# Attention over a graph: scores from turned gathered rows against 16 targets times 4 heads, turned head products kept in f32, four buffers of gathered rows

## The reference, cut to what matters

```python
h = jnp.maximum(_layernorm(x, axis=-1), 0.0)
Q = (h @ Wq).reshape(n, H, D)
K = (h @ Wk).reshape(n, H, D)
V = (h @ Wv).reshape(n, H, D)
score = jnp.einsum('ehd,ehd->eh', Q[src], K[dst]) / np.sqrt(D)
attn = jax.nn.softmax(score, axis=1)          # over the 4 heads
m = V[src] * attn[:, :, None]
h_new = jax.ops.segment_sum(m, dst, num_segments=n)
x = x + layernorm(h_new.reshape(n, H * D) @ Wo + h) * gamma + beta
```

## Time and profile before

| | us |
|---|---|
| median of 3 runs | 3534.71 |
| the runs | 3491.54, 3534.71, 3550.27 |
| profiled execution, its span | 3529.8 |
| PE / DVE / ACT / POOL busy in it | 1964.1 / 2235.0 / 1128.3 / 1615.5 |

### The profile page before, as it was taken

One profiled execution on the slowest core, in us unless ns is written; L12 is line 12 of the kernel. 1 busy time (PEld: TensorE's weight loads), 2 busy tenths in 40 slices (PEclk: granted clock), 3 DMA queues, 4 the chain that ended last, 5 costly groups with the idle time before them and its releaser, 6 DMA issues. The chain is left out here.

```text
span 3529.8 us, 59565 instructions
## 1 busy us (share of the span) xinstructions
PE 1964.1 (56%) x16222; PEld 1430.6 (41%) x16222; DVE 2235.0 (63%) x4872; ACT 1128.3 (32%) x3658; POOL 1615.5 (46%) x1665
## 2 busy tenths in 40 slices
PE   6844555555555555545766556564545445564487
PEld 5723333333333333334344435453434434554222
DVE  7877777777777777754521112134547557987899
ACT  1144555444444444533210111000001001117544
POOL 1055555555555555553666666645666562000000
PEclk9955555555555555556767677675657657985699
DMA  7912121121212222236222222215544432220000
GB/s 240 364 40 45 42 45 43 43 43 44 45 40 45 42 45 41 45 88 224 65 49 50 50 50 48 60 44 154 147 132 145 127 81 84 85 82 0 0 0 9
DMA packets 399309, 267.13 MB, mean 76 GB/s; under 512 B 321456, under 2 KB 349293, under 8 KB 399073
## 3 DMA queue, kind: packets, MB, share of 16 engines
q1 hardware_dynamic: 306278, 87.81, 11.6%
q10 hardware_dynamic: 41472, 118.96, 9.3%
q0 software_dynamic: 51488, 59.40, 6.7%
HBM read 158.59 MB, written 107.47 MB: 75 GB/s over the span
## 5 line engine op out<-in xcount | busy, mean ns | idle before, releaser
L1254 POOL DMA_INDIRECT sorted_edges<-r_load,r_to x800 | 818.6, 1023 | 544.9 <-SPq L1188 310.2
L807 POOL DMA_INDIRECT hsrc<-h,edges x808 | 775.7, 960 | 593.8 <-PE ps L1004 362.4
L1004 PE MATMUL ps<-AO,hsrc 125*64 125x64 f32 x1616 | 195.9, 316 | 309.9 <-remote 254.3
L1049 PE MATMUL ps<-hot,lo 125*128 125x400 bf16 (+2 forms) x1000 | 272.8, 455 | 100.5 <-DVE hot L866 79.9
L1004 PEld LDWEIGHTS ps<-AO,hsrc 125*64 125x64 f32 x1616 | 180.0, 224 | 345.8 <-issue 345.8
L1031 PE MATMUL ps<-rwin,there 120*125 120x256 bf16 x800 | 183.2, 404 | 235.3 <-DVE there L850 220.0
L875 DVE TENSOR_TENSOR prod<-ps,hsrc 125x1024 f32<-125x1024 f32 x200 | 244.3, 1222 | 105.1 <-issue 101.0
L1572 ACT ACTIVATE w_work<-w_work 128x384 f32<-128x384 f32 (+1 forms) x160 | 85.8, 536 | 701.5 <-DVE w_work L1773 530.4
L866 DVE TENSOR_SCALAR hot<-ramp,small 125x400 bf16<-125x400 int16 x800 | 211.9, 322 | 148.0 <-issue 142.7
L1426 PE MATMUL ps<-R 128*128 128x64 bf16 x3000 | 156.6, 218 | 184.5 <-DVE R L1762 115.9
L1031 PEld LDWEIGHTS ps<-rwin,there 120*125 120x125 bf16 x800 | 145.1, 209 | 274.1 <-issue 274.1
(11 more groups left out here) (412 smaller groups left out, 4187.1 us busy)
## 6 DMA issues: line engine op xcount, KB each, us to landing
w_work<-sorted_edges ACTq DMA_DIRECT2D x42, 1000.0 KB
r_load<-in_edge_attr_dram SPq DMA_DIRECT2D x80, 312.5 KB
dstrow<-dst_rows SPq DMA_DIRECT2D x101, 234.4 KB
sorted_edges<-A ACTq DMA_DIRECT2D x10, 2000.0 KB, 9.7
A<-counts SPq DMA_DIRECT2D x12, 1600.0 KB
counts<-A ACTq DMA_DIRECT2D x4, 4000.0 KB, 29.8
sorted_edges<-A ACTq DMA_DIRECT2D x15, 1000.0 KB, 9.5
hsrc<-h,edges POOLq DMA_INDIRECT x808
```

The source lines that it names most:

```text
L807: g.indirect_dma_start(out=hsrc[:, s, t, :], out_offset=None, in_=S.h0[:, :], in_offset=bass.IndirectOffsetOnAxis(ap=edges.bitcast(I32)[:, ...
L1004: mm = pe.matmul(sums.rearrange("d (h w) -> d h w", h=H)[:, :, OFF[t]:OFF[t] + SUB], hsrc[0:TP, s, t, :], AO[0:TP, t, :, :], start=(t == 0 ...
L1049: mm = pe.matmul(S.ps[:, at0 + c0:at0 + c1], lo[0:TP, s, t, :], hot[0:TP, t, c0 - k0:c1 - k0], start=(t == FIRST[k]), stop=False, skip_gro ...
L1254: g.indirect_dma_start(out=S.sorted, out_offset=bass.IndirectOffsetOnAxis(ap=to[:, hf, t:t + 1], axis=0), in_=load[:, hf, t, :], in_offset ...
```

## The change

- **Another way to the scores.** PE turns the gathered rows: 4 transposes of 125 x 128 (two tiles side by side, line 951 of the new program) put the 64 features of two tiles on 128 partitions. ACT copies the 500 columns from PSUM to `hT`. PE then multiplies each tile's turned rows (64 x 125 weights, on the lower or upper 64 partitions by turns) by 16 targets times 4 heads of R: 8 f32 matmuls with 64 columns (line 960). DVE picks for each edge its own target with the 0/1 position `at` (two instructions of 256 elements) and sums over 16 (one of 512 elements). `there`, `dstrow`, the products with `hsrc`, their sums, and ACT's share of them are gone.
- **R turned, in f32.** The first stage now makes R with features on partitions and nodes along the row, keeps it in f32 as `rt`, on both halves of the partitions, and does not split it.
- **Four buffers** of gathered rows, `edges` and `spot`; POOL gathers up to three items ahead. The loop bodies of all engines hold four items, so each engine jumps back 24 times.

The diff, cut:

```diff
-    rwin = sb("rwin", [KW, 2, H * D], BF16)
-    hsrc = sb("hsrc", [P, 2, T, D], F32)
-    there = sb("there", [KW, GE], BF16)
+    rwin = sb("rwin", [P, 2, H, W], F32)
+    hsrc = sb("hsrc", [P, Q, T, D], F32)
+    hT = sb("hT", [P, HT, TP], F32)
...
             with sp.Fori(0, n) as j:
-                for s in range(2):
-                    i = j * 2 + s
-                    g, b = begin(i, s)
+                for s in range(Q):
+                    i = j * Q + s
+                    b = begin(i, s)
                     sp.wait_ge(q["window_free"], i + 1)
-                    sp.dma_start(rwin[:, s, :], S.r3[bass.ds(b, W)].rearrange("n s c -> (n s) c")).then_inc(q[f"rwin{s}"], 16)
-                    line(g, i)
+                    sp.dma_start(rwin[:, s % 2, :, :], S.rt[:, :, bass.ds(b, W)]).then_inc(q[f"rwin{s % 2}"], 16)
...
-                    keys(0, 4)
-                    products(0)
-                    keys(4, 8)
-                    summed = sums(0)
...
-                    products(1)
-                    summed = sums(1)
+                    for t in range(T):
+                        v.wait_ge(q["hot_free"], T * i + t + 1)
+                        v.tensor_scalar(hot[0:TP, t, :], S.ramp[0:TP, OFF[t] * NB:OFF[t] * NB + SK], key[:, t:t + 1], None,
+                                        ALU.is_equal).then_inc(q["hot"], 1)
...
+                    v.wait_ge(q["scores"], i + 2)
+                    for r in range(2):
+                        v.tensor_tensor(prod[0:TP, r:T:2, :, :], scores_at(odd, r).rearrange("p (u h w) -> p u h w", u=HT, h=H),
+                                        at[0:TP, r:T:2, :].unsqueeze(2).to_broadcast([TP, HT, H, SUB]), ALU.mult).then_inc(q["scores_free"], 1)
+                    own.step(v.tensor_reduce(s4, prod[0:TP, :, :, :], AX.X, ALU.add))
+                    own.step(v.tensor_reduce(top, s4, AX.X, ALU.max))
...
+                    act.wait_ge(q["turned"], i + 1)
+                    act.wait_ge(q["scores"], i + 1)
+                    act.copy(hT[:, :, :], S.bank[2 + odd][:, 0:HT * TP].rearrange("p (u e) -> p u e", u=HT)).then_inc(q["moved"], 1)
...
             with pe.Fori(0, n) as j:
-                for s in range(2):
-                    pe.wait_ge(q["there"], i + 2)
...
-                        mm = pe.matmul(S.ps[0:TP, t * 256:(t + 1) * 256], there[:, t * TP:(t + 1) * TP], rwin[:, s, :],
+                for s in range(Q):
+                    for u in range(HT):
+                        if u % 2 == 0:
+                            pe.wait_ge(got[s][u // 2], j * (16 * HT) + 16 * HT)
+                        mm = pe.transpose(S.bank[2 + odd][:, u * TP:(u + 1) * TP],
+                                          hsrc[0:TP, s, 2 * u:2 * u + 2, :].rearrange("p t f -> p (t f)"), S.ident[0:TP, 0:TP])
+                    mm.then_inc(q["turned"], 1)
...
+                    pe.wait_ge(q["moved"], i + 3)
+                    for t in range(T):
+                        rows = slice(t % 2 * D, t % 2 * D + D)
+                        mm = pe.matmul(scores_at(odd, t % 2)[:, t // 2 * H * SUB:(t // 2 + 1) * H * SUB], hT[rows, t // 2, :],
+                                       rwin[rows, odd, :, OFF[t]:OFF[t] + SUB], start=True, stop=True, skip_group_check=True)
+                    mm.then_inc(q["scores"], 1)
                     pe.wait_ge(q["scores"], i + 2)
                     pe.sem_inc(q["window_free"], 1)
-                    weigh(i, 1 - s)
+                    weigh(i, (s - 1) % Q)
...
-                    act.copy(R3[:, c, 0, :], S.bank[4 + c % 3][:, 0:H * D]).then_inc(q["hi"], 1)
-                    act.wait_ge(q["rem"], c + 1)
-                    act.copy(R3[:, c, 1, :], rest[:, c % KQ, :]).then_inc(q["mid"], 1)
+                    act.copy(RT[:, :, c * P:(c + 1) * P], S.bank[4 + c % 3][:, 0:2 * P].rearrange("p (k n) -> p k n", k=2)
+                             ).then_inc(q["rt"], 1)
...
-                    pe.matmul(S.bank[4 + n % 3][:, 0:H * D], HT[0:D, n % KQ, :], Mk[0:D, :], start=True, stop=True).then_inc(q["r"], 1)
+                    for k in range(2):
+                        mm = pe.matmul(S.bank[4 + n % 3][:, k * P:(k + 1) * P], Mk[0:D, k * P:(k + 1) * P], HT[0:D, n % KQ, :],
+                                       start=True, stop=True)
```

More of the change, by code:

```diff
@@ L53 @@
 SP3 = 3
-KW = SP3 * W
+Q = 4
 KEYS = NB * W
@@ L737, in attend @@
     q = {n: sem("a_" + n) for n in (
-        "spot0", "spot1", "edges0", "edges1", "rwin0", "rwin1", "dstrow", "zero", "spot_free", "window_free",
-        "there", "lo", "squares", "lo_free", "hot", "hot_free", "scores", "scores_free", "soft", "expo", "ao", "ao_free", "carrier",
-        "edges_free", "counted", "count_free", "u", "u_free", "zeros", "proj", "proj_free", "own", "summed")}
-    got = [[sem(f"a_got{s}{t}") for t in range(T)] for s in range(2)]
-    STEPS = 10
+        "rwin0", "rwin1", "zero", "spot_free", "window_free",
+        "lo", "squares", "lo_free", "hot", "hot_free", "turned", "moved", "scores", "scores_free", "soft", "expo", "ao", "ao_free", "carrier",
+        "edges_free", "counted", "count_free", "u", "u_free", "zeros", "proj", "proj_free", "own")}
+    spotted, landed = ([sem(f"a_{n}{s}") for s in range(Q)] for n in ("spot", "edges"))
+    got = [[sem(f"a_got{s}{hf}") for hf in range(2)] for s in range(Q)]
+    STEPS = 8
     half = NB * NP // 2
@@ L835, in _ @@
             v.wait_ge(q["zero"], 5)
-            def place(own, n, s, seen):
-                v.wait_ge(q[f"spot{s}"], seen)
-                own.did(v.tensor_scalar(thr[0:KW, :], S.thirdf[0:KW, :], spot[0:KW, s, 1:2], None, ALU.add))
-                v.wait_ge(q[f"edges{s}"], seen)
-                own.did(v.tensor_scalar(near[0:TP, :, :], edges[0:TP, s, 0:2, :], spot[0:TP, s, 1:2], None, ALU.subtract))
-                v.wait_ge(q["window_free"], n + 2)
-                v.wait_ge(q["dstrow"], n * 16 + 16)
-                own.settle()
-                v.tensor_scalar(there[:, :], dstrow[:, :], thr[0:KW, :], None, ALU.is_equal).then_inc(q["there"], 1)
-                own.did(v.scalar_tensor_tensor(key, near[0:TP, 0, :], float(NB), edges[0:TP, s, 2, :], ALU.mult, ALU.add))
@@ L853, in _, with place @@
-            place(first, 0, 0, 16)
-            with v.Fori(0, pairs_of(v)) as j:
-                for s in range(2):
-                    i = j * 2 + s
-                    own = Own(v, q["own"], j * (2 * STEPS + 2) + s * STEPS + 5)
+            def place(own, s, seen):
+                v.wait_ge(spotted[s], seen)
+                v.wait_ge(landed[s], seen)
+                own.step(v.tensor_scalar(near[0:TP, :, :], edges[0:TP, s, 0:2, :], spot[0:TP, s, 1:2], None, ALU.subtract))
+                own.did(v.scalar_tensor_tensor(key, near[0:TP, 0, :], float(NB), edges[0:TP, s, 2, :], ALU.mult, ALU.add))
@@ L858, in _ @@
+            place(first, 0, 16)
+            with v.Fori(0, quads_of(v)) as j:
+                for s in range(Q):
+                    i, odd = j * Q + s, s % 2
+                    pair = j * (Q // 2) + s // 2
+                    own = Own(v, q["own"], j * (Q * STEPS + Q) + s * STEPS + 2 * (s // 2) + 4)
                     th = "p (t h) -> p t h"
-                    four = [TP, HT, H, D]
+                    four = [TP, T, H, SUB]
                     s4, e4, a4 = (x.rearrange(th, h=H) for x in (score, expo, attn))
-                    def keys(t0, t1):
-                        for t in range(t0, t1):
-                            v.wait_ge(q["hot_free"], T * i + t + 1)
-                            v.tensor_scalar(hot[0:TP, t, :], S.ramp[0:TP, OFF[t] * NB:OFF[t] * NB + SK], key[:, t:t + 1], None,
-                                            ALU.is_equal).then_inc(q["hot"], 1)
@@ L869, in products @@
-                    def products(hf):
-                        v.wait_ge(q["scores"], 2 * i + hf + 1)
-                        v.wait_ge(q["summed"], 2 * i + hf + 2)
-                        for t in range(HT):
-                            v.wait_ge(got[s][HT * hf + t], j * 16 + 16)
-                        v.tensor_tensor(prod[0:TP, :].rearrange("p (t h f) -> p t h f", t=HT, h=H),
-                                        S.ps[0:TP, hf * 1024:(hf + 1) * 1024].rearrange("p (t h f) -> p t h f", t=HT, h=H),
-                                        hsrc[0:TP, s, HT * hf:HT * (hf + 1), :].unsqueeze(2).to_broadcast(four),
-                                        ALU.mult).then_inc(q["scores_free"], 1)
@@ L951, in bring_sums @@
                          S.ps[0:D, 3072:3072 + H * W].rearrange("d (h w) -> d h w", h=H)[:, :, 0:SEEN]).then_inc(q["u_free"], 1)
-            def rows(n, s, seen):
-                act.wait_ge(q[f"edges{s}"], seen)
-                act.wait_ge(q["lo_free"], n + 1)
-                for t in range(T):
-                    op = nc.scalar.activation(lo[0:TP, s, t, :], S.ramp[0:TP, 0:P], ACT.Square, bias=edges[0:TP, s, 3, t:t + 1])
-                op.then_inc(q["squares"], 1)
-                act.wait_ge(q["squares"], n + 1)
```

(1 more changed line is left out.)

255 lines of the change are left out of this document (104 added, 151 removed).

## The result

| | before | changed |
|---|---|---|
| median us | 3539.68 (4 runs) | 3725.06 (4 runs) |
| lowest to highest | 3491.54 to 3550.27 | 3716.61 to 3752.53 |
| ratio, 95% interval | | 1.0604 (1.0528 to 1.0679) |

The changed kernel is 6% slower; 3420 us was forecast. A later set of runs has it **3% faster**: 3021.13 us against 3108.84, ratio 0.971 (0.9689 to 0.9731). Both are real, and the difference between them is the finding of this study: in some sets of runs the engines are held up while POOL gathers, in others they are not.

The account below looks back on a forecast made before the run. The prediction took a ring of waits to bound the attention stage, with no engine full. PE's period of 12.4 us against 13.54, times 100 items, gave -114 us: 3416, so 3420 us by the median; range 3250 to 3570.

Parts of the forecast that it names:

- the price of the jump back: PE's loop in the attention stage: 4.1 us per trip, now once in four items, so 1.0 us per item.
- The scores: PE's 16 f32 score matmuls per item: a pitch of 0.221 us, 3.74 us in all, 1.94 as lower bound.
- I keep the 12%: PE's clock in the attention stage: granted 0.56, so 12% of the time at 2.4 GHz, taking 1.1 us off.
- PE's period: PE's time per item in the attention stage: 11.45 us plus 1.0 for the jump back, 12.4 us.
- POOL's* floor: POOL's gathers in the attention stage: 10.0 us plus a quarter of a jump back, 10.6 us per item.
- at no cost for the 512 pieces: SP's rwin DMA moving 512 pieces of 160 B instead of 120 rows: costed at nothing, being issued two items ahead.
- below the rest: SP's work in the attention stage: some 9 us per item, less than the other engines need.
- a sign of being wrong that the prediction named: The forecast is wrong if SP's DMAs come late, or PE waits for ACT's copy much longer than 0.8 us.
- The first stage at no cost: First stage, making R: equal columns on PE, so costed at nothing, with bounds of 10 us saved or lost.
- B: Rival: POOL becomes the bound at 10.6 to 11.2 us per item, 3241 to 3301 us; chance 0.20.
- D: Rival: slower, the stall at PE's jump grows with the loop's body to 13.7 us a trip, 3666 us; chance 0.16.
- C's clock of 0.50: Rival: no change, PE's clock stays at 0.50 for the whole stage, 13.6 us per item, 3541 us; chance 0.26.

Follow-up runs that it names:

- no_gather: The changed kernel without its gathers, POOL only counting the rows as brought: 3098.05 us, where the kernel before took 3604.96.
- sp_early_again: The changed kernel with SP bringing the next item's spot and edges before its window wait and reading group and start from SBUF: 3692.83 us.
- after_again: The changed kernel run once more, unedited, in a set with stalls: 3795.30 us, where the kernel before took 3621.30.
- set 3: Runs with stalls, kernel before 3621.30 us; the changed kernel with its window read in 128 pieces took 3797.76 us, with 512 pieces 3795.30.
- half_rows: The changed kernel with each gather bringing 64 rows instead of 128, in a set without stalls: 3002.47 us.

## Why the prediction was wrong

**The step that failed is the reading of PE's stall as the price of the jump back** ("The jump back thus costs the path 4.1 us per trip", and from it "now comes once in four items: 1.0"). The kernel before without stalls has the same jumps and no such stall. What it was: PE was held while POOL gathered. The term put at 1.0 us per item was 5.0 us, and four items in a trip save nothing, since the stall comes with each item's gathers. That gathers are the cause is shown for the changed kernel (no_gather); for the kernel before it is read from the same signs, since it never ran without gathers in a set with stalls. Two signs could be seen before: in the trace the stall ended 2.0 us behind POOL's last gather, and SP needed 2.86 us from one DMA to the next, which I took for SP's pace. PE's 5.2 us, DVE's 2.94 us and SP's 2.86 us look like one thing, since all three are gone in the profile without stalls; I priced them as three.

**Why the changed kernel pays twice.** Without stalls it is 11.13 to 10.22 us per item, 0.91 less. With them it is 13.50 to 15.21, so they cost the kernel before 2.4 us per item and the changed one 5.0. (The stages behind lose 176 and 178 us more, which is why the kernel before itself goes from some 3120 to 3540 us.) In the kernel before, each batch of gathers slows SP as well, but PE stands still for it only once in two items; in the other it waits for DVE's `there` (4.1 us) in any case. In the changed kernel an item needs PE's completions for ACT's copy, for the scores, DVE's products, `u` and the window, with nothing else to wait for, and the stall is on the path each time. Its four buffers also let POOL gather without a pause, as at 204 to 234 us. SP's late `edges` add about 1.0 us of the 5.0 (sp_early_again against after_again). All but these 1.0 us is read from the traces, not shown by a run of its own.

**The terms.** *PE.* The scores were over-sized: 16 records take 1.95 us at the granted 0.50 and 1.09 us at 1.00, not 3.74, a pitch of 0.10 us, not 0.221. These 1.8 us too many hide part of what the stall lacks in the sum. Transposes, copy, weighing, counts and project came as said. *The clock.* "I keep the 12%" was wrong where PE is not held: without gathers it is granted 0.74, with them and no stalls 0.71; with stalls 0.58. Together PE's period is 8.75 us and not 12.4. *POOL's* floor, 10.6 us, is 10.2. *DVE:* products 420 ns each and the sum 686, as the groups of the profile after show:

```profile
L833 DVE TENSOR_TENSOR prod<-ps,at 125x256 f32<-125x256 f32 x200 | 75.6, 420 | 201.1 <-remote 166.7
L836 DVE TENSOR_REDUCE small<-prod 125x32 f32<-125x512 f32 x100 | 68.6, 686 | 3.4
L892 ACT COPY hT<-ps 128x500 f32<-128x500 f32 x100 | 57.6, 576 | 542.8 <-PE ps L951 379.6
```

against 0.4 each and 0.65; ACT's copy 576 ns against 586. *SP* at no cost for the 512 pieces: right (set 3); "below the rest" was wrong where the stalls are, since its `edges` come late there, a sign of being wrong that the prediction named. The first stage at no cost: right, 146.32 us of PE against 143.90 in the same 214 us; the 20 us by which the first weighing comes later (236.96 against 216.60) are the first hold.

**The rivals.** B (0.20) is what the kernel does without stalls, by its mechanism (POOL the bound) and by its reason: the score matmuls alternate between lower and upper 64 partitions, and 16 of them cost half of what the pitch of the earlier trace rows gives. The Trainium skill ("TensorE: Matmul & The Clock Gate", Part 3) has a weight load overlap the matmuls in flight if its row group differs; the 1.95 us agree with it, though no run had them all in one row group. D (0.16) gave nearly the time, 3666 us, by a stall that grows with the loop's body; no_gather has the longer body, the same jumps and no stall, so that mechanism is out and the near time is luck. C's clock of 0.50 was not seen.

**What stays open.** What holds PE and SP, and why only at times: 3621.30 and 3120.31 us for the kernel before on the same chip in two sets. No packet moves on the instruction queue from 279 to 1792 us of the profile after, nor from 238 to 1576 us of the one before, so it is not code loading; the gather's transfers take the same time with stalls and without (median 0.116 us for 2 KB). Whether the rows or the gather instructions count (half_rows), how the kernel before does without gathers in a set with stalls, and the pitch of 1.36 us there weren't answered.

## What to carry to other kernels

A stall that ends on nothing in the kernel belongs to no line until something has been taken away: look for what ended just before it, and for the other engines' slow instructions in the same microseconds, before it is priced as a loop's jump. A kernel that gathers should be timed in more than one set of runs, with the old kernel beside it each time, since a change can lose 6% in one and win 3% in the next. A stage that no edit touches tells, run by run, which kind of run it was. Where such stalls are present, fewer gathers per microsecond can be the faster choice; where they are not, it costs.

## What the runs showed of the hardware

- Eight gathers of 128 rows of 256 B, 1.25 us apart, hold back other engines from about 4 us after the first until about 2 us after the last, in some sets of runs: SP's register instructions (187 of 618 in that stretch, in the kernel before) take 0.70 us instead of 0.04, and completions of matmuls, as the profile models them, reach the waiting engines mostly 3 to 8 us late, once 17 us behind 24 gathers in a row. With a pitch of 1.50 us PE's unexplained waits are halved (200 us instead of 410 from 400 to 1480 us). In other sets it is absent at any pitch tried, 1.25 to 1.76 us.
- f32 matmuls with 125-wide weights on alternating halves of the partitions: 0.10 us of pitch at the granted 0.50, against 0.22 us for eight of 128-wide weights and 66 columns on one half.
- A gather of 64 rows mostly takes POOL 0.90 us, one of 128 rows 0.95.
- The same work of PE ran at a granted clock of 0.74 without gathers (busy 436.61 of 600 us), at 0.71 with gathers and no stalls (394.82 of 600) and at 0.58 with the stalls (753.28 of 1546).
